# Two sequence tiles share one block in both attention stages of a two-layer transformer step

## What is computed

```python
xn = layernorm(x)
q, k, v = xn @ Wq.T, xn @ Wk.T, xn @ Wv.T
decay = sigmoid(xn @ Wd.T + bd)
diff = pos[None, :] - pos[:, None]             # source - target
weights = exp(log(decay) * clip(diff - 1, 0)) * (diff > 0)
x = x + ((q @ k.T * scale) * weights) @ v @ Wo.T * out_scale \
      + xn @ int4(kernel) + bias + (xn @ a) @ b
xn = layernorm(x)
# layer 1: a linear recurrence, written in the kernel as masked products over the
# whole sequence, with mask gamma ** (t - 1 - s) for s < t
x = x + alpha * reads @ W_read.T \
      + relu(xn @ ternary(W1).T + b1) @ ternary(W2).T + b2
```

## Time and profile before

| | |
|---|---|
| median of 3 runs | 1641.5 us (1577.0 to 1736.6) |
| profiled execution, whole | 1579.6 us |
| its span, slowest core (core 6) | 1578.1 us |
| spans of the 8 cores | 1547.7 to 1578.1 us |
| TensorE busy | 1235.3 us, 78% |
| ScalarE / VectorE busy | 474.9 / 418.6 us |
| mean granted TensorE clock, core 6 | 0.913 |
| layer 0 tiles 0 to 3 begin | 371.9, 486.7, 597.2, 696.0 us |
| layer 1 tiles 0 to 3 begin | 885.5, 1036.2, 1202.6, 1383.3 us |

### The profile page before, as it was taken

One profiled execution on the slowest core, in us unless ns is written; L12 is line 12 of the kernel. 1 busy time (PEld: TensorE's weight loads), 2 busy tenths in 40 slices (PEclk: granted clock), 3 DMA queues, 4 the chain that ended last, 5 costly groups with the idle time before them and its releaser, 6 DMA issues. The chain is left out here.

```text
span 1578.1 us, 15265 instructions; the slowest of 8 cores (1547.7 to 1578.1 us)
## 1 busy us (share of the span) xinstructions
PE 1235.3 (78%) x5332; PEld 535.4 (34%) x5440; DVE 418.6 (27%) x704; ACT 474.9 (30%) x550; POOL 137.4 (9%) x184
## 2 busy tenths in 40 slices
PE   0275289996796587664559999979997999899997
PEld 0121034442342232221224444434443444334443
DVE  1497435002223324323167300030002100031000
ACT  1564033334424625626113341014202140031400
POOL 2331100000110211202200000000000000000000
PEclk9988589997898887886869999989998999999999
DMA  8795953002425636647492442244234142331422
GB/s 196 115 170 90 141 74 53 1 0 87 127 80 193 182 115 220 207 176 207 129 184 41 149 152 80 101 186 134 88 125 187 47 141 83 121 143 57 130 107 107
DMA packets 74202, 194.42 MB, mean 123 GB/s; under 512 B 8272, under 2 KB 16496, under 8 KB 69776
## 3 DMA queue, kind: packets, MB, share of 16 engines
q0 software_dynamic: 37072, 105.34, 27.8%
q1 hardware_dynamic: 37056, 88.09, 17.5%
HBM read 195.57 MB, written 33.56 MB: 145 GB/s over the span
## 5 line engine op out<-in xcount | busy, mean ns | idle before, releaser
L1183 PE MATMUL pb<-bigA,wqA 128*128 128x512 bf16 x1002 | 224.7, 379 | 1.2
L1143 PE MATMUL pb<-xn,xbf 128*128 128x512 bf16 x1004 | 221.5, 380 | 1.1
L1126 PE MATMUL pb<-stm,bigB 128*128 128x512 bf16 x627 | 144.8, 390 | 35.1 <-DVE xa_bf L999 27.7
L1084 ACT ACTIVATE bigA<-pb,cstF 128x512 bf16<-128x512 f32 x128 | 99.5, 777 | 217.8 <-PE pb L1143 217.8
L1165 PE MATMUL pb<-rt,projW 128*128 128x512 bf16 x501 | 125.4, 391 | 46.6 <-DVE rt L1004 41.5
L1034 DVE SCALAR_TENSOR_TENSOR xf<-pb,cstF,xf 128x512 f32<-128x512 f32 x32 | 24.0, 751 | 479.5 <-PE pb L1183 479.5
L1143 PEld LDWEIGHTS pb<-xn,xbf 128*128 128x128 bf16 x1024 | 100.2, 98 | 121.7
L1183 PEld LDWEIGHTS pb<-bigA,wqA 128*128 128x128 bf16 x1024 | 100.1, 98 | 120.9
L1126 PEld LDWEIGHTS pb<-stm,bigB 128*128 128x128 bf16 x640 | 63.3, 100 | 116.6 <-issue 47.1
L1113 PE MATMUL pb<-xn 128*128 128x512 bf16 x313 | 75.7, 403 | 31.6 <-PEq L924 29.5
L429 PE MATMUL pb<-rt,cstB 128*128 128x512 bf16 x110 | 34.8, 445 | 82.9 <-DVE rt L395 82.9
(11 more groups left out here) (129 smaller groups left out, 1140.0 us busy)
## 6 DMA issues: line engine op xcount, KB each, us to landing
wqA<-W2qS POOLq DMA_DIRECT2D x32, 1024.0 KB, 5.1
xbf<-W1qS SPq DMA_DIRECT2D x128, 256.0 KB, 2.6
xbf<-W2T SPq DMA_DIRECT2D x26, 512.0 KB, 4.0
bigA<-W2T POOLq DMA_DIRECT2D x32, 256.0 KB, 9.2
bigA<-W1T POOLq DMA_DIRECT2D x16, 512.0 KB, 9.7
xf<-xT SPq DMA_DIRECT2D x4, 2048.0 KB, 9.0
x1S<-xf POOLq DMA_DIRECT2D x4, 2048.0 KB, 8.4
stm<-W1T SPq DMA_DIRECT2D x16, 512.0 KB, 5.1
```

Source lines behind the costliest of these rows:

```text
L1084: got = si(s.activation(bigA[:, fc * 512:(fc + 1) * 512], pb[fc % 2][:, :], AF.Relu, bias=biasL[:, 48 + fc:49 + fc], scale=sc[:, C_Q4:C_Q4 ...
L1126: got = ti(t.matmul(bank[:, :], bigB[:, i * 1024 + ec * 128: i * 1024 + (ec + 1) * 128], stm[:, i * 512:(i + 1) * 512], start=(n == 0), st ...
L1143: got = ti(t.matmul(bank[:, :], xbf[:, (fc % 4) * 1024 + dc * 128: (fc % 4) * 1024 + (dc + 1) * 128], xn[:, p0:p0 + TS], start=(dc == 0), ...
L1183: got = ti(t.matmul(bank[:, :], wqA[:, (dc % 2) * 4096 + fc * 128: (dc % 2) * 4096 + (fc + 1) * 128], bigA[:, fc * 512:(fc + 1) * 512], st ...
```

## The change

`attn_tile` no longer opens a block of its own. It is given one, and the four tiles of each layer run as two pairs, (0, 1) and (2, 3), a block for each pair. So the joins between tiles 0 and 1 and between 2 and 3 of both layers are gone (four), and those between 1 and 2 stay. The second tile of a pair receives `prev`, the semaphore counts of the first, and waits explicitly where the join had made it safe. Matmuls, vector, scalar and DMA work are the same, in the same order on each engine. Apart from indentation the diff is:

```diff
-    def attn_tile(layer, j):
+    def attn_tile(layer, j, blk, prev):
...
-        with nc.Block() as blk:
 @blk.sync
+                def qld_issue(h):
+                    if prev and not stm_gd[0] and (h % NSL) >= 2:
+                        s.wait_ge(sT, prev["t_R"][7])
+                        stm_gd[0] = True
+                    q_qld[h] = qld_q(h)[0](s, qldF(h), q_src(h))
...
                     if fc >= 4:
                         s.wait_ge(sT, t_h[fc - 4])
+                    elif prev:
+                        s.wait_ge(sT, prev["t_h"][28 + fc])
 @blk.vector
+            if prev:
+                v.wait_ge(sS, prev["s_last"] if layer == 0
+                          else prev["s_mask"][-1])
+                v.wait_ge(sT, prev["t_R"][7])
             for idx, i in enumerate(schunks):
...
 emit_mask
             if idx >= 4:
                 s.wait_ge(sV, v_mult[idx - 4])
+            elif prev:
+                s.wait_ge(sV, prev["v_mult"][prev["NS"] - 4 + idx])
 @blk.tensor
             if layer == 0:
+                if prev:
+                    t.wait_ge(sV, prev["v_R"][4])
                 ... xa ...
             for idx, i in enumerate(schunks):
                 if idx >= 4:
                     t.wait_ge(sV, v_mult[idx - 4])
+                elif prev:
+                    if layer == 0:
+                        pw = [("v", prev["v_res"][6]), ("v", prev["v_res"][7]),
+                              ("v", prev["v_mult"][prev["NS"] - 2]),
+                              ("v", prev["v_mult"][prev["NS"] - 1])][idx]
+                    else:
+                        pw = [("s", prev["s_h"][30]), ("s", prev["s_h"][31]),
+                              ("v", prev["v_res"][6]),
+                              ("v", prev["v_res"][7])][idx]
+                    t.wait_ge(sV if pw[0] == "v" else sS, pw[1])
...
                 if ec >= 4:
                     t.wait_ge(sV, v_R[ec - 4])
+                elif prev:
+                    t.wait_ge(sV, prev["v_R"][ec + 4])
 @blk.gpsimd
                     if dc >= 2:
                         g.wait_ge(sT, t_res[dc - 2])
+                    elif prev:
+                        g.wait_ge(sT, prev["t_res"][6 + dc])
...
-    for j in range(NTT):
-        attn_tile(0, j)
+    for jp in ((0, 1), (2, 3)):
+        with nc.Block() as blk:
+            prevt = None
+            for j in jp:
+                prevt = attn_tile(0, j, blk, prevt)
     PROJ1()
     (the same for layer 1)
```

More of the change, by code:

```diff
@@ L922, in attn_tile @@
             s_h = [s0 + NS + fc + 1 for fc in range(NFC)]
-        with nc.Block() as blk:
[L925 to L929, removed]
-            if layer == 1:
[L931 to L1018, removed]
@@ L1090, in _ @@
-            @blk.tensor
-            def _(t):
-                if layer == 0:
+            else:
+                for idx, i in enumerate(schunks):
+                    v.wait_ge(sT, t_st[idx])
+                    v.wait_ge(sS, s_mask[idx])
+                    got = vi(v.tensor_mul(
+                        stm[:, i * 512:(i + 1) * 512], pb[idx % 4][:, :],
+                        maskb[:, (idx % 4) * 512:(idx % 4) * 512 + 512]))
+                    assert got == v_mult[idx]
+                for ec in range(8):
+                    v.wait_ge(sT, t_R[ec])
+                    got = vi(v.tensor_scalar_mul(
+                        rt[:, ec * 512:(ec + 1) * 512], pb[4 + ec % 4][:, :],
+                        sc[:, C_ALPHA:C_ALPHA + 1]))
+                    assert got == v_R[ec]
+                for dc in range(8):
+                    v.wait_ge(sT, t_res[dc])
+                    v.wait_ge(sQs, q_x[0])
+                    got = vi(v.scalar_tensor_tensor(
+                        xf[:, dc * 512:(dc + 1) * 512], pb[2 + dc % 2][:, :],
+                        biasL[:, 40 + dc:41 + dc],
+                        xf[:, dc * 512:(dc + 1) * 512], ALU.add, ALU.add))
+                    assert got == v_res[dc]
@@ new lines, in emit_mask @@
+        def emit_mask(s, idx):
+            i = schunks[idx]
+            s.wait_ge(sV, prefA[idx])
+            if idx >= 4:
+                s.wait_ge(sV, v_mult[idx - 4])
+            elif prev:
+                s.wait_ge(sV, prev["v_mult"][prev["NS"] - 4 + idx])
+            mslot = maskb[:, (idx % 4) * 512:(idx % 4) * 512 + 512]
+            if strad(i):
+                k = i - 4 * j
+                got = si(s.activation(mslot, statsB[:, k * 512:(k + 1) * 512],
+                                      AF.Exp, bias=biascols[:, i:i + 1]))
+            else:
+                scl = (ld_cols[:, i:i + 1] if layer == 0
+                       else sc[:, C_NLG:C_NLG + 1])
+                got = si(s.activation(mslot, Bcs[:, :], AF.Exp,
+                                      bias=biascols[:, i:i + 1], scale=scl))
+            assert got == s_mask[idx]
@@ L1116, in _ @@
[L1116 to L1125 removed]
+                        p0 = xnp(dc, j * TS, 1)
                         got = ti(t.matmul(
@@ L1150, in _ @@
[L1150 to L1164 removed]
+                            xbf[:, (fc % 4) * 1024 + dc * 128:
+                                 (fc % 4) * 1024 + (dc + 1) * 128],
@@ new lines, in _ @@
+                            xn[:, p0:p0 + TS],
+                            start=(dc == 0), stop=(dc == NDC - 1)))
+                    assert got == t_h[fc]
+            rb = 0 if layer == 0 else 2
+            for dc in range(8):
+                if dc == 0:
+                    t.wait_ge(sV, v_mult[NS - 1])
+                    t.wait_ge(sV, v_R[7])
+                    if layer == 1:
+                        t.wait_ge(sS, s_h[NFC - 1])
+                if dc >= 2:
+                    t.wait_ge(sV, v_res[dc - 2])
+                if layer == 1:
+                    t.wait_ge(w2q_q[dc % 2][1], exp_w2[dc])
+                bank = pb[rb + dc % 2]
+                first = True
+                got = None
+                for ec in range(8):
+                    got = ti(t.matmul(
+                        bank[:, :],
+                        projW[:, ec * 1024 + dc * 128: ec * 1024 + (dc + 1) * 128],
+                        rt[:, ec * 512:(ec + 1) * 512],
+                        start=first, stop=False))
+                    first = False
+                if layer == 0:
+                    for d2 in range(8):
+                        p0 = xnp(d2, j * TS, 0)
@@ L1213, in build_nc @@
-    for j in range(NTT):
-        attn_tile(0, j)
-    PROJ1()
-    for j in range(NTT):
-        attn_tile(1, j)
+                            wqA[:, d2 * 1024 + dc * 128: d2 * 1024 + (dc + 1) * 128],
+                            xn[:, p0:p0 + TS], start=False, stop=False))
+                    got = ti(t.matmul(bank[:, :],
+                                      b_sb[0:16, dc * 128:(dc + 1) * 128],
+                                      xa_bf[0:16, :], start=False, stop=True))
+                else:
+                    for fc in range(NFC):
+                        got = ti(t.matmul(
+                            bank[:, :],
+                            wqA[:, (dc % 2) * 4096 + fc * 128:
+                                 (dc % 2) * 4096 + (fc + 1) * 128],
+                            bigA[:, fc * 512:(fc + 1) * 512],
+                            start=False, stop=(fc == NFC - 1)))
@@ new lines, in _ @@
+                assert got == t_res[dc]
+        @blk.gpsimd
+        def _(g):
+            if layer == 1:
+                for dc in range(8):
+                    if dc >= 2:
+                        g.wait_ge(sT, t_res[dc - 2])
+                    elif prev:
+                        g.wait_ge(sT, prev["t_res"][6 + dc])
+                    got = w2q_q[dc % 2][0](g,
+                        wqA[:, (dc % 2) * 4096:(dc % 2) * 4096 + 4096],
+                        bass.AP(W2qS.tensor, dc * 128 * 4096,
+                                [[4096, 128], [1, 4096]]))
+                    assert got == exp_w2[dc], (dc, got, exp_w2[dc])
+            if layer == 0:
+                for h in range(NH):
+                    if h >= 4:
+                        g.wait_ge(qst_q(h - 4)[1], q_qst[h - 4])
+                    g.wait_ge(sV, cmb_tok[h])
+                    q_qst[h] = qst_q(h)[0](g, q_dst(h), qout(h))
+                    assert q_qst[h] == exp_qst[h], (h, q_qst[h], exp_qst[h])
+            g.wait_ge(sV, v_res[7])
+            dst = x1S if layer == 0 else outT
+            qgD(g, tile_dst(dst, j), xf[:, :])
@@ L1221, in build_nc @@
+    PROJ1()
+    for jp in ((0, 1), (2, 3)):
+        with nc.Block() as blk:
+            prevt = None
+            for j in jp:
+                prevt = attn_tile(1, j, blk, prevt)
     with nc.Block() as blk:
```

331 lines of the change are left out of this document (167 added, 164 removed).

## The result

The changed kernel takes 1545.9 us (median of 9 executions, lowest 1541.2), the kernel before 1575.5 us beside it (median of 10). The ratio is 0.981, with a 95% interval of 0.979 to 0.982: 1.9% faster, 30 us. 28.1 us were forecast. (Single executions took up to 1756 us changed and 1737 us before, in the changed kernel with one die at a mean granted clock of 0.79 instead of 0.92; the 1641.5 us shown before was one of these, none of them was profiled, and the ratios leave them out.)

The account below looks back on a forecast made before the run. TensorE, busy 78%, was taken to bound layer 1, the quantization ring layer 0. Gains of 23.7 us in layer 1 and 4.4 in layer 0 sum to 28.1: 1579.6 - 28.1 = 1551.5 us, range 1538 to 1618.

Parts of the forecast that it names:

- Layer 1, both joins, 23.7 us: Layer 1 tiles 1 and 3: TensorE's idle time and slow start go, 11.65 and 12.5 us, less 0.2 per tile.
- The bias work: VectorE at the start of layer 1 tiles 1 and 3: costs nothing; if exposed, at most 3.75 us per tile.
- Why a join costs 10 us: At a tile's end the join waits for POOL's store of `xf` to land, 7.5 us in layer 1, and adds 0.7.
- The slabs: The `W1qS` loads in layer 1 tile 1 land in time for `h`, by 3 us or more.
- slabs late: Rival, chance 0.12: `wqA` loads beside the store delay the layer 1 slabs; TensorE waits 3 to 4 us; 1557 us.
- a sign of being wrong: Named among the signs against the forecast: a landing of the `outT` store above 8 us.
- Layer 0, 4.4 us: Layer 0 tiles 1 and 3, held by the quantization ring, gain only 2.5 and 1.9 us; bounds 1.5 and 5.1.
- the root of tile 1: Layer 0 tile 1: the ring's first load moves 0.9 us earlier, q0's sum 3.1 us; 2.5 us taken.
- Where TensorE's time goes in layer 0: Time freed by the joins returns as idle time before `R` and `res`, growing by nearly 10 us a tile.
- Layer 0 gains fully: Rival, chance 0.13: the quantization ring doesn't bind, so layer 0 gains up to 24.8 instead of 4.4 us; 1531 us.
- The clock doesn't hold: Rival, chance 0.07: TensorE's clock falls beyond 171 us of unbroken work, 319 us exposed; at 0.84 it is 1611 us.
- The range: Total time from 1538, called half of what layer 0 could gain more, to 1618, over late slabs, little change and clock.

Follow-up runs that it names:

- the two experiments above: Changed kernel with TensorE waiting in layer 1 for the store's landing: ratio 0.998; kernel before with SP instead of POOL storing `xf`: ratio 0.976.
- e7: Changed kernel plus a TensorE wait, in layer 1 tiles 1 and 3, for the previous store of `xf` to land: ratio 0.998 to the kernel before.
- e5: Changed kernel with SP's first three or four quantization loads in layer 0 issued before its wait for the store of `xf`: 1528.2 us, ratio 0.972.
- e6: Changed kernel with all four tiles of a layer in one block and the first quantization loads ahead of SP's wait for the store: 1504.9 us, ratio 0.957.
- 630 us in the experiment: Changed kernel with all four tiles of a layer in one block instead of two pairs: 1532.1 us, ratio 0.972 to the kernel before.

## Why the prediction was right, step by step

*Layer 1, both joins, 23.7 us.* Right. Measured 11.7 + 12.2 = 23.9, where the sum had 11.65 and 12.5 before 0.4 was taken off. The idle times and the slow starts are both gone, and the experiment that kept only the wait brought both back. The bias work cost nothing, as reckoned.

*Why a join costs 10 us.* Right in mechanism: it waits for POOL's store. I had read it from two sums of issue and landing; the two experiments above show it in both directions, and POOL's DRAIN in the trace ends with the landing. A join with nothing to wait for costs 1.8 us, which the landing hides here but for the 0.7 us of the prediction.

*The slabs.* They were to be in time by 3 us or more; they were by 7. The rival "slabs late" took the worst case of store and `wqA` loads one behind the other, 17.1 us. The store took 8.3 instead of 7.5 us, over the 8 us that I had named as a sign of being wrong. It cost nothing, since the slabs had the 7 us to spare. The interleaving that the Trainium skill tells of ("DMA: Bandwidth & Descriptors", "Issuing engines are not separate DMA queues") agrees with what is seen: side by side both took longer, the store by 0.8 us and the `wqA` loads by 2.4 (12.0 against the 9.6 beside SP's `xf` load before), though both are POOL's here. The worst case, the one behind the other, did not occur.

*Layer 0, 4.4 us.* Right in mechanism, too small by the stages: 4.6 + 1.9 = 6.5 us, above my upper bound of 5.1. The pairs in layer 0 alone gave 4.8 us on the medians, within it, so part of the excess can be noise. The mis-sized term is the root of tile 1. I had 0.9 us for the load and another 2.2 for q0's sum, 3.1, and took 2.5. Measured as a mean of the cores, the Signs came 1.6 us earlier and the sum closed up by another 2.7, together 4.3, and all of it reached `res`, so nothing was to be taken off. In e7, with the same layer 0, only 2.9 us reached `res`. I had read core 6, where the store took 8.4 us to land; the mean was 7.7. After the change SP starts 7.5 to 7.6 us behind the store's issue on every core. Tile 3 was met (1.9), but in part by luck: I took 2.0 us for q0's sum, and it came 1.0 us earlier, `res` 1.2.

*Where TensorE's time goes in layer 0.* I had said before `R` and `res`, and that the idle time there would grow by nearly 10 us a tile. Before `res` it shrank, by 1.6 and 1.4 us. In tile 3 9.2 us went inside `R`, whose groups wait for VectorE's copies to free their banks. In tile 1 3.8 us went before `R` and 4.2 into `st` itself: the groups st10 and st11 wait 3.7 and 0.8 us for products whose masks stand behind Signs in ScalarE's list. That was to be read in the written-out order and I didn't. It costs nothing, since `R` is late in any case, waiting for the copy of `xa` behind q5 in VectorE's list.

*The kept joins.* Tile 2 of layer 0 gained 1.3 us, for which the sum had nothing. In layer 0 the cores differ by up to 7 us in that tile, and the experiments with the layer 0 joins kept or gone have it at 94.9 and 95.1, so I don't count this as an effect of the change.

*The rivals.* "Layer 0 gains fully" was wrong for this change but right as a place to look: 17 us more are there behind the order of SP's list (e5), and 25 with all four tiles in one block (e6). "The clock doesn't hold": 1.00 over 334 us after the change and over 630 us in the experiment. Its exposed stretch was too long to begin with: before the change TensorE already worked from 815.7 to 1026.5 us, 211 us with no pause over 1.8 us, at 1.00, and not 171 at most; and the first pair is 296 us long, where the 305 had not been shortened by the gain. The warning in the Trainium skill ("TensorE: Matmul & The Clock Gate", "Seeing it yourself") of 13/16 of the clock under dense matmuls on three or more cores of a die is not borne out in any of the profiled executions, with eight cores at work.

*The range.* Its lower end, 1538, was called half of what layer 0 could gain more; half of the way from 1551.5 to 1531 is 1541. Nothing hangs on it.

*The 2%.* The forecast was 1.8%, the result 1.9% with an interval of 1.8 to 2.1%, so on either side of that bound, most of it below.

## What to carry to other kernels

In this kernel a join of engines waited for a store that POOL had under way, and not for one of SP. Before you remove joins, look whether a store is issued just ahead of them, and from which engine. Moving these stores to SP was worth 40 us, more than removing four of the joins (30 us), and takes a few lines.

Where a stage hangs on a ring of load, compute and store, its start counts: 7.9 and 11.1 us at the root moved `res` by 8.4 and 8.0 us. Look for what stands ahead of its first load in the issuing engine's list, and for large transfers beside its first stores. When two things hold the same load, taking away either brings nothing (0.1 and 0.9 us in tile 2), and both together 10 us.

## What the hardware showed that I had not expected

- A block's end waited for a 2 MB store issued by POOL (9.5 to 10.8 us idle at a tile's join) and did not wait for the same store issued by SP (1.8 us idle, store landed 9.2 us after its issue). POOL's DRAIN took 8.0 us there, SP's 0.13.
- After 9.7 to 10.3 us of idle time TensorE lost 1.9 to 2.6 us to a slow start; after 1.83 us it ran at 1.00 and lost nothing that counts (25 matmuls in 5.58 us, 0.2 us over 25 x 0.216).
- Two 1 MB loads issued by POOL right behind its 2 MB store went with a landing of the store after 8.3 us instead of 7.5 (8.0 to 8.6 us on all eight cores), while the loads themselves took 12.0 us, against 9.6 beside SP's 2 MB load before.
- A 256 KB store took 3.2 us to land, and 3.9 to 7.3 us (means of the cores) where a 2 MB load was under way beside it. That the load is the cause was not tested.
